# A graph attention layer on one core: one written-out first stage, and the key branch moved into the attention steps

## Time and profile before

| | |
|---|---|
| median of 3 runs | 3508.43 us (3499.73 to 3509.04) |
| the profiled execution | 3502.63 us, its span 3500.8 us |
| PE, DVE, ACT, POOL busy | 81%, 66%, 44%, 45% |
| the page's 40 slices | the first stage is the first 3.6 of them, attention ends in the 28th |
| DMA | 300 MB, 86 GB/s in the mean; 213 MB of them by the gathers' queue |

### The profile page before, as it was taken

One profiled execution on the slowest core, in us unless ns is written; L12 is line 12 of the kernel. 1 busy time (PEld: TensorE's weight loads), 2 busy tenths in 40 slices (PEclk: granted clock), 3 DMA queues, 4 the chain that ended last, 5 costly groups with the idle time before them and its releaser, 6 DMA issues. The chain is left out here.

```text
span 3500.8 us, 62646 instructions
## 1 busy us (share of the span) xinstructions
PE 2851.8 (81%) x18287; PEld 2146.4 (61%) x18287; DVE 2294.9 (66%) x6128; ACT 1525.3 (44%) x4088; POOL 1569.7 (45%) x1641
## 2 busy tenths in 40 slices
PE   3773667777787788787878888886999999999999
PEld 2562555666666666666767677674666566566565
DVE  6773666777687787787888888883454444435434
ACT  0221444555455455565555565652333333333332
POOL 0223777777777777777777777740000000000000
PEclk7886777778778878888888888877999999999999
DMA  3222444444444444444444444434010100101000
GB/s 114 75 85 62 119 115 116 119 120 119 116 121 119 116 125 117 115 124 116 125 117 121 119 122 122 118 85 147 1 43 1 43 12 31 43 1 42 1 11 11
DMA packets 145375, 300.13 MB, mean 86 GB/s; under 512 B 30480, under 2 KB 78608, under 8 KB 144912
## 3 DMA queue, kind: packets, MB, share of 16 engines
q0 software_dynamic: 75552, 212.96, 23.4%
q1 hardware_dynamic: 61392, 74.37, 6.8%
q10 hardware_dynamic: 8096, 8.82, 0.8%
HBM read 260.39 MB, written 35.65 MB: 85 GB/s over the span
## 5 line engine op out<-in xcount | busy, mean ns | idle before, releaser
L791 POOL DMA_INDIRECT xg<-edge_table,idx x1568 | 1495.0, 953 | 509.3 <-issue 490.4
L997 PE MATMUL ps_y<-y,hotw 128*128 128x260 f32 x3520 | 904.0, 423 | 45.4 <-issue 44.8
L997 PEld LDWEIGHTS ps_y<-y,hotw 128*128 128x128 f32 x3520 | 723.9, 214 | 207.7 <-issue 51.6
L1350 ACT ACTIVATE h<-ps_h,bnb,bns 128x448 f32<-128x448 f32 x448 | 324.6, 724 | 624.2 <-PE ps_h L1310 624.2
L1452 DVE SCALAR_TENSOR_TENSOR yb<-ps_ye,wts,yb 128x256 f32<-128x256 f32 x392 | 189.7, 484 | 576.6 <-PE ps_ye L1318 576.6
L897 ACT ACTIVATE y<-xg,w 128x65 f32 x1760 | 468.9, 338 | 7.5 <-ACT w L889 0.4
L1142 DVE TENSOR_TENSOR y<-xg,ps_v 128x780 f32<-128x780 f32 x440 | 418.0, 960 | 8.5 <-DVE ps_v L1136 0.5
L912 ACT CAST hotw<-hot 128x512 f32<-128x512 bf16 x440 | 267.4, 622 | 230.6 <-PE ps_y L997 230.3
L1310 PE MATMUL ps_h<-zt,w 128*128 128x448 f32 x896 | 362.6, 560 | 6.3 <-issue 6.0
L1318 PE MATMUL ps_ye<-wo,h 128*128 128x256 f32 x1568 | 348.1, 379 | 0.0
L1310 PE MATMUL ps_h<-h,w 128*128 128x448 f32 x896 | 345.9, 539 | 0.0
(11 more groups left out here) (234 smaller groups left out, 3239.1 us busy)
## 6 DMA issues: line engine op xcount, KB each, us to landing
xg<-edge_table,idx POOLq DMA_INDIRECT x1568
mix_rows<-mixed SPq DMA_DIRECT2D x55, 257.0 KB
t<-mix_rows SPq DMA_DIRECT2D x7, 1799.0 KB, 7.7
xb<-xn_turned SPq DMA_DIRECT2D x55, 128.0 KB
edge_table<-rows ACTq DMA_DIRECT2D x7, 924.0 KB, 4.2
x<-in_x SPq DMA_DIRECT2D x7, 896.0 KB, 6.9
xn_turned<-xnt SPq DMA_DIRECT2D x7, 896.0 KB, 4.9
x7e<-in_x SPq DMA_DIRECT2D x7, 896.0 KB, 9.8
```

The lines of the kernel that those rows point to most:

```text
L791: pool.indirect_dma_start(xg[:, q * OCT + u, j, :], None, dr["table"], bass.IndirectOffsetOnAxis(ap=idx[q][:, c:c + 1], axis=0)).then_inc( ...
L997: mm = pe.matmul(ps_y[v % 2][:, 0:RW], hotw[v % 2][:, j, :], y[v % 2][:, j, :], start=(j == 0), stop=(j == CH - 1))
L1350: act.activation((h1, h2)[layer][:, mh, half * HN:(half + 1) * HN], ps_h[g % 4][:, 0:HN], ACT.Relu, bias=K.bnb[:, layer, c:c + 1], scale=K ...
```

## The change

`edge_lists`, `weights` and `project` become one `Block`, `prepare`, written out for seven chunks. Per block it normalises on ACT (one activation with scale and bias), turns `xn` on PE, copies it on ACT, multiplies with `wcat`, and DVE adds the product and a row of constants straight into `acc`, whose rows now hold the head columns, ones, and the eight score columns (AW = 268), in place of `rows7` and `state`. SP stores `xn` as well as the turned `xn`. The table is stored from `acc`. List and weight work is put between blocks at written-out places. Indices are kept as int16.

The key branch is done in attention in 25 pairs of blocks (KP), four (PRE) before step 0, and 21 in steps 0 to 20, each through the bank of the queries (`ps_q`) and spare columns of `ps_y[0]`: sums are added in SBUF by DVE. In step 21 they become `kvw`. The 49 query blocks go to steps 22 to 54, one and two in turn: the second has its products behind the second visit of the y loop and its mix behind the fifth. `dlist` has one buffer instead of two.

```diff
+KP = -(-NB // 2)
+PRE = 4
+FIN = KP - PRE
...
+for c in range(NI):
+    q = c % 2
+    sp.wait_ge(xn_d, ONE + (c + 1) * IB)
+    sp.dma_start(nodes(dr["xn"], c * IB, IB), xn7[q][:]).then_inc(xn_stored[q], 16)
+    if c + 2 < NI:
+        load(c + 2)
+    sp.wait_ge(xnt_d, ONE + (c + 1) * IB)
+    sp.dma_start(dr["xnt"][whole(c)].rearrange("j p c -> p j c"),
+                 xnt7[q][:].rearrange("p j k n -> p j (k n)")).then_inc(xnt_stored[q], 16)
+    if c == 1:
+        for t in range(VT):
+            sp.wait_ge(rows_in[t], 16)
+            sp.dma_start(dr["dst"][t * P:t * P + rows[t], :], xrows[0:rows[t], t, 0:GE]).then_inc(stored, 16)
...
+pe.wait_ge(consts_in, 32)
+for j in range(IB):
+    turn(0, j)
+count_blocks()
+pe.wait_ge(wcat_d, ONE + 1)
+for c in range(NI):
+    for j in range(IB):
+        rows_of(c, j)
+        if c + 1 < NI:
+            turn(c + 1, j)
+        if (c, j) == (0, 2):
+            turn_groups()
+        if (c, j) == (1, 5):
+            turn_weights()
+        if j == 4 and T0 <= c < T0 + VT:
+            turn_lists(c - T0)
+        if (c, j) == (NI - 1, 4):
+            fold_weights()
...
+def norm(c, j):
+    b = c * IB + j
+    if j == 0:
+        act.wait_ge(nmr_d, ONE + c + 1)
+        if c > 1:
+            act.wait_ge(xn_stored[c % 2], 16 * (c // 2))
+            act.wait_ge(turned, ONE + (c - 1) * IB)
+    act.activation(xn7[c % 2][:, j, :], x7[c % 2][:, j, :], ACT.Identity,
+                   bias=var[:, 2, b:b + 1], scale=var[:, 1, b:b + 1]).then_inc(xn_d, 1)
+def keep(c, j):
+    b = c * IB + j
+    if j == 0 and c > 1:
+        act.wait_ge(xnt_stored[c % 2], 16 * (c // 2))
+        act.wait_ge(proj_d, ONE + (c - 1) * IB)
+    act.wait_ge(turned, ONE + b + 1)
+    act.copy(xnt7[c % 2][:, j, :, :].rearrange("p k n -> p (k n)"), ps_t[b % 2][:, 0:2 * P]).then_inc(xnt_d, 1)
+def store(c, lo, hi):
+    act.wait_ge(rows_d, ONE + c * IB + hi)
+    act.dma_start(nodes(dr["table"], c * IB + lo, hi - lo), K.acc[:, c * IB + lo:c * IB + hi, 0:TW]).then_inc(table_stored, 16)
...
+for c in range(NI):
+    if c + 1 < NI:
+        norm(c + 1, 0)
+    for j in range(IB):
+        if c + 1 < NI:
+            if j + 1 < IB:
+                norm(c + 1, j + 1)
+            keep(c + 1, j)
+        if c > 0 and j == 1:
+            store(c - 1, 0, IB)
+        if c == NI - 1 and j == 4:
+            store(c, 0, 4)
+        if j == 5 and c + 2 < NI:
+            root(c + 2)
...
+def row(c, j):
+    b = c * IB + j
+    dve.wait_ge(proj_d, ONE + b + 1)
+    dve.tensor_tensor(K.acc[:, b, :], ps_p[b % 2][:, 0:AW], one_row[:], ALU.add).then_inc(rows_d, 1)
...
+reach()
+for j in range(IB):
+    stat(0, j)
+variance(0)
+rstd(0)
+gat_columns()
+for j in range(IB):
+    stat(1, j)
+variance(1)
+groups()
+rstd(1)
+for c in range(NI):
+    if T0 <= c < T0 + VT:
+        casts(c - T0)
     for j in range(IB):
+        row(c, j)
+        if c + 2 < NI:
+            for k in (2 * j, 2 * j + 1):
+                if k < IB:
+                    stat(c + 2, k)
+            if j == 4:
+                variance(c + 2)
+            if j == IB - 1:
+                rstd(c + 2)
+        if (c, j) == (0, 4):
+            indices()
+        if (c, j) == (1, 2):
+            freed()
+        if (c, j) == (1, 4):
+            breaks()
+        if (c, j) == (1, 6):
+            words()
+        if (c, j) == (T0 + 1, 1):
+            value_weights()
+        if (c, j) == (T0 + 1, 6):
+            centre()
+        if (c, j) == (4, 0):
+            batch_norms(0)
+        if (c, j) == (5, 0):
+            batch_norms(1)
+    if T0 <= c < T0 + VT:
+        spreads(c - T0)
+folded()
...
+def pair_at(s):
+    return PRE + s if s < FIN else None
+def mixes(s):
+    n = s - FIN - 1
+    if n < 0:
+        return ()
+    b = n + n // 2
+    return (b, b + 1) if n % 2 else (b,)
+def width(p):
+    return min(2, NB - 2 * p)
...
+p = pair_at(n(1))
+if p is not None and p + 1 < KP:
+    turned_in(p + 1)
+    plain_in(p + 1)
+if n(1) == FIN:
+    block_in(0)
+for b in mixes(n(1)):
+    if b + 1 < NB:
+        block_in(b + 1)
+    mixed_out(b)
...
+keyed, blocks = pair_at(n(1)), mixes(n(1))
+if keyed is not None:
+    square(keyed)
+if n(1) == FIN:
+    act.wait_ge(col_d, ONE + KP)
+    act.activation(root[:, 0:2], col[:, 2:4], ACT.Sqrt).then_inc(root_d, 1)
+if blocks:
+    fourth(blocks[0])
 for p in range(2, SV // 2):
     turned(p, n)
+if keyed is not None:
+    normed(keyed)
...
+        if v == 0 and blocks:
+            mix_copy(blocks[0])
+        if len(blocks) == 2 and v == 2:
+            fourth(blocks[1])
+        if len(blocks) == 2 and v == 5:
+            mix_copy(blocks[1])
+def square(p):
+    act.wait_ge(kb_d, ONE + p + 1)
+    for k in range(width(p)):
+        at = ps_q[:, k * D:(k + 1) * D]
+        sq = act.activation(at, at, ACT.Square, accum_out=ks[:, 0, k:k + 1])
+    sq.then_inc(k2_d, 1)
+def normed(p):
+    act.wait_ge(kr_d, ONE + p + 1)
+    act.wait_ge(ka_d, ONE + p)
+    for k in range(width(p)):
+        at = ps_q[:, k * D:(k + 1) * D]
+        act.activation(kn[:, k, :], at, ACT.Copy, scale=ks[:, 2, k:k + 1])
+        sq = act.activation(kk[:, k * D:(k + 1) * D], at, ACT.Square, scale=ks[:, 2, k:k + 1])
+    sq.then_inc(kn_d, 1)
...
+if keyed is not None:
+    keys(keyed)
+if n(1) == FIN:
+    values()
+if blocks:
+    queries(blocks[0])
...
+if keyed is not None:
+    pe.wait_ge(acc_d, ONE + n(SV))
+    gram(keyed)
+if blocks:
+    mix(blocks[0])
...
+if len(blocks) == 2 and v == 1:
+    queries(blocks[1])
+if len(blocks) == 2 and v == 4:
+    mix(blocks[1])
...
+def keys(p):
+    pe.wait_ge(xk_in, 16 * p + 16)
+    pe.wait_ge(kas_d, ONE + p)
+    for k in range(width(p)):
+        for kh in range(2):
+            mm = pe.matmul(ps_q[:, k * D:(k + 1) * D], xb[:, k, kh * P:(kh + 1) * P], K.wk[:, kh, :],
+                           start=(kh == 0), stop=(kh == 1))
+    mm.then_inc(k_d, 1)
+def gram(p):
+    pe.wait_ge(xn_in, 16 * p + 16)
+    pe.wait_ge(kn_d, ONE + p + 1)
+    pe.wait_ge(col_d, ONE + p)
+    last = width(p) - 1
+    for kh in range(2):
+        for k in range(last + 1):
+            pe.matmul(ps_q[:, kh * D:(kh + 1) * D], xnk[:, k, kh * P:(kh + 1) * P], kn[:, k, :],
+                      start=(k == 0), stop=(k == last))
+    for kh in range(2):
+        for k in range(last + 1):
+            pe.matmul(ps_y[0][:, RW + kh:RW + kh + 1], kn[:, k, kh * P:(kh + 1) * P], one[:],
+                      start=(k == 0), stop=(k == last))
+        for k in range(last + 1):
+            mm = pe.matmul(ps_y[0][:, RW + 2 + kh:RW + 3 + kh], kk[:, k * D + kh * P:k * D + (kh + 1) * P], one[:],
+                           start=(k == 0), stop=(k == last))
+    mm.then_inc(ka_d, 1)
...
+    if v == 1 and keyed is not None:
+        dve.wait_ge(py_d, ONE + n(SV) + 1)
+        columns(keyed)
     add_up(v - 1, blk[v - 1], n)
+if v == 2 and keyed is not None:
+    sums_up(keyed)
+if v == 2 and n(1) == FIN:
+    values()
...
+def sums_up(p):
+    dve.wait_ge(ka_d, ONE + p + 1)
+    at = ps_q[:].rearrange("p (k c) -> p k c", c=D)
+    if p == 0:
+        dve.tensor_copy(ats[:], at).then_inc(kas_d, 1)
+    else:
+        dve.wait_ge(kas_d, ONE + p)
+        dve.tensor_tensor(ats[:], ats[:], at, ALU.add).then_inc(kas_d, 1)
...
+for p in range(PRE):
+    bias(p)
+    build(p, 0, 0)
+    scales(p)
+    columns(p)
+    sums_up(p)
...
-        edge_lists(nc, io, dr, K, W)
-        weights(nc, K, W)
-    project(nc, io, dr, K)
+K.wk, K.bk, K.bvw = ml.sb("wk", [P, 2, D]), ml.sb("bk", [P, D]), ml.sb("bvw", [P, D])
+prepare(nc, io, dr, K)
```

More of the change, by code:

```diff
@@ new lines, in indices, with breaks @@
+                def indices():
+                    dve.wait_ge(gt_d, ONE + VT)
+                    for t in range(VT):
+                        link(dve.tensor_copy(gidx[0:rows[t], t:t + 1], ps_g[0:rows[t], t * P:t * P + 1]))
+                    dve.engine_nop().then_inc(gidx_d, 1)
+                def breaks():
+                    link(dve.memset(same[:, 0:1], 0.0))
+                    link(dve.tensor_tensor(same[:, 1:NVT], blkf[:, 1:NVT], blkf[:, 0:NVT - 1], ALU.is_equal))
+                    link(dve.memset(same[:, 0:NVT:SV], 0.0))
+                    link(dve.tensor_scalar(same[:], same[:], -1.0, BIG, ALU.add, ALU.mult))
+                    link(dve.tensor_copy(K.brk[:], bc(same[:].rearrange("p (s v) -> p s v", v=SV), 2, HEADS)))
@@ new lines, in _ @@
+                link(dve.memset(one_row[:], 0.0))
+                link(dve.memset(one_row[:, HD:RW:HC], 1.0))
+                link(dve.memset(wcat[:, :, HD:RW:HC], 0.0))
+                dve.memset(ones[:], 1.0).then_inc(ones_set, 1)
+                dve.memset(xrows[:, :, GE:GE + 1], 0).then_inc(rows_set, 1)
+                dve.memset(lastf[:, GE - 1:GE], 1.0).then_inc(last_d, 1)
+                reach()
+                for j in range(IB):
+                    stat(0, j)
+                variance(0)
@@ L708, in attend @@
         y = [m.sb(f"y{q}", [P, CH, RW]) for q in range(2)]
```

(14 more changed lines are left out.)

861 lines of the change are left out of this document (372 added, 489 removed).

## The result

The changed kernel takes 3343.03 us (median of four runs, 3340.92 to 3351.58) against 3505.31 us of the kernel before beside it: a ratio of 0.9544 (0.9530 to 0.9558), 162 us faster. Forecast were 3338 us. The profiled execution took 3340.92 us, its span 3339.1.

What follows compares the result with a forecast made beforehand. POOL's gathers were taken to bound attention, behind a serial first stage. Span 3500.8 - 176 (first stage) + 2 (preamble) + 10 (late steps) = 3337 us, so 3338 us measured time; range 3308 to 3360, 8 in 10 3308 to 3385.

Steps and rivals of the forecast that it cites:

- POOL's pace bounds attention: Attention: 1568 gathers on POOL, 1.283 us each, set the pace, so a shorter first stage moves everything behind it equally.
- Rival C: Attention: each gather takes longer, from key loads or DVE instructions in the way; 3573 us at 0.15 us each; chance 0.03.
- First gather at 142 us: End of the first stage: first gather at 142 us instead of 318.3, gaining 176 us; likely 125 to 170.
- rival B: First stage: stalls on transfers, loads 4 us later in five loops, first gather at 165 to 175, 3360 to 3375 us; chance 0.14.
- ACT's normalising at 0.37 to 0.42 us: First stage: price of ACT's normalising of one block, taken from today's copies and squares.
- what leaves the first stage: First stage: list of key work per chunk, POOL's two 4 us additions, end sums and barriers; an old chunk takes 33 us.
- Preamble: Attention before step 0: four key pairs take 58 us, ready 61 us after opening; step 0 17 us late, costing 2 us.
- The ring: Attention's gather slots: POOL waits for a released slot if step 0 is late; 0 to 8 us, taken as 2.
- Steps 0 to 20 cover the key pairs: Attention, steps 0 to 20: key pairs in place of query blocks add 3 us a step, hidden at no cost.
- Steps 22 to 54: +10 us: Late attention: second query blocks make steps 34.5 us against 33.7 of gathers, adding 10 us at the end; bounds 0 to 77.
- The 4.8 us to spare: End of attention: slack of the last step, 3.93 + 0.9 us, subtracted from 14.5 us of lag.
- Rival A: Late attention: steps become engine-bound, ACT's waits vanish from step 22 on, +40 us, 3370 to 3400 us; chance 0.13.

Runs made afterwards that it cites:

- e11: The changed kernel with DVE building the one-hot matrices from a bf16 row of numbers in SBUF instead of f32 in PSUM: 3377.1 us, ratio 0.9653.
- e3: The changed kernel with three buffers of x in the first stage instead of two: 3338.7 us, ratio 0.9537.
- e6: The changed kernel with six key pairs before step 0 instead of four, and two-block steps first, then one-block steps: 3345.5 us, ratio 0.9550.
- e7: The changed kernel without the key branch in attention, its matrix a constant: 3343.6 us, ratio 0.9546.
- e9: The kernel before the change with POOL's additions in the project stage left out, POOL only signalling: 3443.1 us, ratio 0.9842.

## Why the prediction was right, point by point

- **POOL's pace bounds attention, and a shorter first stage moves all behind it.** Right: the last gather is earlier by 184.7 us, and the gathers were not slowed. Rival C fell; e11 shows that its second mechanism, DVE in the way of POOL, is real where a DVE instruction with both inputs in SBUF overlaps a gather. The key branch did not bring it on: 25 gathers take over 1 us, 26 did before.
- **First gather at 142 us.** Measured 145.9 (141.5 to 147.1 over seven executions). Constants and visit numbers were awaited until 16.7 us, not 13, and the first row came at 33.5 in place of 31. The waits for x were as put: 2.05 and 5.05 us in the first two loops, 0.6 later; rival B's transfers did not hold the stage, which moved 386 GB/s from 50 to 60 us; e3 shows what the waits for x cost, 5 us. "DVE fuller than PE" was wrong: 83.6 and 83.7 us busy. PE fell to half clock in more places than I had (0.77 granted from 100 to 120 us), from 50 us on each time behind a wait of 2.1 to 7.4 us for DVE's rows. In the second row below four products take 2.13 us, where they take 1.07 at the full clock:

```profile
49.97 0.75 DVE L435 BATCH_NORM_STATS2 stats<-x 128x6 f32<-128x256 f32 x2 [5.05 <-DMA x<-in_x]
...
51.21 2.13 PE L291 MATMUL ps_p<-wcat,xnt 128*128 128x268 f32 x4 [3.90 <-DVE acc L454]
```

- **ACT's normalising at 0.37 to 0.42 us** was mis-sized; the view of the line, below, has 601 ns. The Trainium skill, "ScalarE: Activation LUTs", What ACT_TABLE_LOAD costs, gives 186 ns plus 0.833 for each column plus 93 for each operand by pointer: an estimate of 585 ns for 256 columns with scale and bias, which the trace bears out. It cost nothing here, ACT being busy 46 us of 146.

```profile
L385 ACT ACTIVATE xn<-x,var x49: 584/601/608, 22.4 to 120.7; 128x256 f32<-128x256 f32 x49
```

- **Why before was at 318 us.** My account of what leaves the first stage listed POOL's additions as work beside the path, and did not ask why L628 took 1455 ns where L664, of the same shape, took 349. It did no harm to the sum, since the new stage was costed from below and not as a difference, but a cause of 53 us was not named.
- **Preamble.** Step 0's scores ended 55 us behind the opening (61 forecast, 44 before). The ring did not hold POOL: the 65th gather started as its slot came free, within a microsecond or two. e6 shows that there is no slack left behind it.
- **Steps 0 to 20 cover the key pairs.** Right (e7).
- **Steps 22 to 54: +10 us, measured +25.4.** This is the term that failed, in its size. The surcharge of a second block was put too high (4.5 forecast, 3.2 measured). The own time of a step was put too low, and that weighs more, since it counts in every step: I took 32.3 us, a mean over steps of which most had waited for a gather. In steps 38 to 53 of before, the nine that waited over 1 us took 31.1 us besides the wait, the five that did not wait 33.0. That engines catch up during a wait would explain it; no run here tests that. A one-block step of the changed kernel waits for nothing and takes 33.6 us, which the one such pair in the earlier trace rows had shown too. With 33.6 and 36.8, mean 35.15 in steps 38 to 54, against the gathers' 33.7, the lag is 1.45 x 17 = 25 us. The 4.8 us to spare that I took off did not show. ACT's waits were gone from step 38, as said, and the waits in all attention fell from 321.1 us to 110.7. Rival A (+40) was nearer in kind than I gave it, though the waits vanished from step 38 on and not from 22, and of its +40 only 25 came. Its +40 was also not twice my +10, as I called it, and the 3363 of rival C lay 3 us outside the forecast's own range, not inside; neither bore on the forecast.
- **The gathers from first to last, 2012 forecast, 2000.1 measured.** Other executions with the changed attention have 2003 to 2007.6 (leaving out e6 and e11), those with attention of before 2009.7, 2012.4 and 2014.7. So some 5 of the 12 us are this execution's luck, and 7 or so are real. Gaps of 0.45 to 2.2 us between gathers are fewer with the changed attention (7 to 15, 6 to 11 us in sum, against 16 to 24, 12 to 19 us). What makes them fewer was not settled; it is not the key pairs (e7: 2005.9).

## What to carry to other kernels

Read an engine-bound step's own time only from steps that waited for nothing: here steps that waited were shorter even without the wait (31.1 against 33.0 us), and a mean over both hides that the slack is gone. Extra work belongs into the steps whose bound leaves the most room; the same block costs 1.0 or 3.1 us of lag by where it stands. Look at least, median and most of a line whenever its mean is far from that of a like instruction: the outlier names an engine that shuts the other one out.

## What the runs showed of the hardware

- A POOL addition of 4.0 us holds a DVE tensor_scalar of 0.40 us for its whole length (4220 ns at most; 414 at most without the additions, e9).
- A DVE tensor_tensor with both inputs in SBUF (bf16, 1.22 us) lengthens an indirect DMA's instruction on POOL from 0.95 to up to 2.0 us, in 108 of 355 that overlap one (e11); with one input in PSUM 2 of 307 are over 1 us (the changed kernel). The bf16 inputs from SBUF made the instruction itself no faster (1219 against 1217 ns).
- POOL idles 0.30 us between two gathers, but once every 112 gathers it idles 2.4 to 3.8 us: at 13 places in the kernel before, at 11 of them in the changed one. No run here shows why.
